# Four fused cross-attention layers on one core: row projection, weights cast in parts, masks moved between engines, three steps on GpSimd, new orders

## The reference

```
# layer 0: 16 heads of 8, causal (k < q, query 0 attends nothing)
x = layer_norm(x + softmax(mask(q k^T / sqrt(8))) v @ Wo + bo) * g1 + b1
x = layer_norm(x + relu(x @ W1 + b1) @ W2 + b2) * g2 + b2
# layer 1: 16 heads of 8, no mask, no norm
x = x + attention(x, ctx) @ Wo + bo
x = x + gelu_tanh(x @ W1 + b1) @ W2 + b2
# layer 2: gate; pooled = mean over tokens of ctx
vis = pooled @ Wv.T + bv;  text = x @ Wt.T + bt
route = softmax over tokens of 2 * sum(text * vis)
gate = sigmoid(text @ Wg_t.T + (route * vis) @ Wg_v.T + bg)
x = layer_norm(x + gate * route * vis) * gamma + beta
# layer 3: 16 heads of 64, on an rms-normed query
x = x + attention(rms_norm(x) * norm_w @ wq, ctx @ wk, ctx @ wv) @ wo
```

## Time and profile before

| | before |
|---|---|
| median of 3 runs | 1521.21 us |
| profiled execution: its span | 1521.7 us |
| PE busy | 1418.5 us (93%) |
| DVE busy | 1080.6 us (71%) |
| ACT busy | 977.0 us (64%) |
| POOL busy | 488.1 us (32%) |
| chain that ended last | PE 76%, DVE 10%, POOL 5%, ACT 4%, issue 4% |

### The profile page before, as it was taken

One profiled execution on the slowest core, in us unless ns is written; L12 is line 12 of the kernel. 1 busy time (PEld: TensorE's weight loads), 2 busy tenths in 40 slices (PEclk: granted clock), 3 DMA queues, 4 the chain that ended last, 5 costly groups with the idle time before them and its releaser, 6 DMA issues.

```text
span 1521.7 us, 48865 instructions
## 1 busy us (share of the span) xinstructions
PE 1418.5 (93%) x20325; PEld 1030.3 (68%) x20325; DVE 1080.6 (71%) x2644; ACT 977.0 (64%) x1877; POOL 488.1 (32%) x522
## 2 busy tenths in 40 slices
PE   4779999999999999999999999999999999999987
PEld 3455766767676676767667676776767667676756
DVE  4558778677786867778676777867687785776743
ACT  2355767667676766767576676767667676665654
POOL 2132523315242341524224252332424233152402
PEclk9999999999999999999999999999999999999998
DMA  4000000000000000000000000000000000000000
GB/s 141 15 2 15 3 8 16 9 16 2 22 3 9 16 9 16 3 22 3 9 16 9 16 3 22 3 9 16 9 16 3 9 16 9 2 3 8 3 8 9
DMA packets 27798, 20.02 MB, mean 13 GB/s; under 512 B 1088, under 2 KB 27200, under 8 KB 27328
## 3 DMA queue, kind: packets, MB, share of 16 engines
q1 hardware_dynamic: 27584, 16.90, 3.8%
HBM read 12.70 MB, written 4.19 MB: 11 GB/s over the span
## 4 chain that ended last, share of the span: by engine, by line
PE 76%; DVE 10%; POOL 5%; ACT 4%; issue 4%; DMA 0%; SPq 0%; ACTq 0%; DVEq 0%
PE bank L731 63%; PE bank L740 13%; DVE negmax L1261 2%; POOL prob L1157 2%; DVE sums L1408 2%; ACT prob L1096 1%; POOL rstd L1144 1%; DVE z L1319 1%; ACT probT L1031 1%; DVE negmax L1402 1%; DVE stats L1305 1%; POOL prob L1137 1%; POOL var_eps L1141 1%; POOL w_low L1128 0%; DVE mv L1310 0%
## 5 line engine op out<-in xcount | busy, mean ns | idle before, releaser
L1137 POOL TENSOR_TENSOR prob<-prob,rinv 128x512 f32<-128x512 f32 x256 | 262.4, 1044 | 369.1 <-DVE rinv L1268 368.7
L740 PE MATMUL bank<-cst,prob 128*128 128x128 f32 x1536 | 221.5, 277 | 14.5 <-POOL prob L1157 9.6
L740 PEld LDWEIGHTS bank<-cst,prob 128*128 128x128 f32 x1536 | 173.9, 141 | 62.5 <-issue 32.7
L1031 ACT ACTIVATE probT<-bank 128x512 f32<-128x512 f32 x256 | 143.8, 598 | 110.3 <-PE bank L740 109.4
L1261 DVE TENSOR_REDUCE negmax<-bank 128x8 bf16<-128x512 f32 x256 | 159.0, 680 | 70.7 <-PE bank L731 70.6
L1157 POOL TENSOR_TENSOR prob<-prob,rinv 128x512 f32<-128x512 f32 x128 | 132.5, 1042 | 230.0 <-DVE rinv L1412 229.7
L1024 ACT ACTIVATE prob<-bank 128x512 f32<-128x512 f32 x256 | 142.0, 608 | 80.3 <-PE bank L731 80.0
L1266 DVE TENSOR_REDUCE sums<-prob 128x8 f32<-128x512 f32 x256 | 169.2, 661 | 12.9 <-ACT prob L1024 11.0
L731 PE MATMUL bank<-negmax,ident_b 128*128 128x512 bf16 x384 | 129.6, 389 | 14.1 <-DVE negmax L1261 8.3
L731 PE MATMUL bank<-wt,Q 128*128 128x128 f32 x1024 | 126.1, 277 | 0.0
L1096 ACT ACTIVATE prob<-bank,rms_rows 128x256 f32<-128x256 f32 x256 | 104.5, 483 | 30.8 <-PE bank L731 30.7
(11 more groups left out here) (155 smaller groups left out, 2968.7 us busy)
## 6 DMA issues: line engine op xcount, KB each, us to landing
x_in<-in_x SPq DMA_DIRECT2D x16, 256.0 KB, 3.0
c_in<-in_ctx SPq DMA_DIRECT2D x16, 256.0 KB, 3.3
out<-y SPq DMA_DIRECT2D x16, 256.0 KB, 2.3
Q<-in_split_weights SPq DMA_DIRECT2D x1, 1536.0 KB, 9.1
wt<-in_weights SPq DMA_DIRECT2D x1, 1024.0 KB, 10.8
wt<-in_weights SPq DMA_DIRECT2D x1, 640.0 KB, 5.9
wt<-in_weights SPq DMA_DIRECT2D x4, 128.0 KB, 10.4
cst<-in_constants SPq DMA_DIRECT2D x1, 229.0 KB, 2.7
```

Source lines behind the costliest of these rows:

```text
L740: last = nc.tensor.transpose(o[:, k * P:(k + 1) * P], src(k), ident)
L1031: nc.scalar.activation(probT[:, t].rearrange("p s q -> p (s q)"), bank(g, "PT", l, u, t)[:, :], ACT.Identity).then_inc(probT_ready.sem, 1)
L1137: nc.gpsimd.tensor_tensor(pr, pr, ri, ALU.mult).then_inc(norm_ready.sem, 1)
```

## The change

- **Row projection.** `o.0` computes rows (tokens on partitions): four matmuls with 128 columns of `aT` as the stationary operand and `Wo0` as the moving one. A new POOL step `xb` adds the bias, spread over all rows, to the loaded rows `x_in`; `attout.0` adds that to the bank into `z[0]`, in rows. `lnT.0` is gone; `stats.0` and `z.0` read `z[0]` in SBUF. `ffn.0` writes `x1T[0]`. SP's load of group g + 1 also waits for `xb(g)`, and `xb(g)` for `attout.0` of the group before.
- **Weights in parts.** ACT casts `wk3` in step `c_high` and `wv3`, `wq3` one after the other in `qm.0`; DVE subtracts for `wk3` in `c_low`, POOL for the other two. `k3`, `v3`, `q3` wait each for its own part.
- **Masked keys by ACT.** Step `km` goes to ACT: two activations with scale and bias, the form of `qm`.
- **Masked values by copies.** `Vm` is zeroed once, and `vm` copies only the heads that the half keeps: two copies of 256 elements per partition.
- **Three steps on GpSimd**: `vis_route`, `y_gamma`, `y_beta`.
- **New orders**: all five lists, and a bank table for each of the 16 groups.

```diff
-TURN = 89.7521
+TURN = 88.5425
...
             def load(g):
...
                     sp.wait_ge(*cT_filled(g))
+                    sp.wait_ge(*xb_ready(g))
                     load(g + 1)
...
@@ PE, step "o" and text_weights
-                    mm(bank(g, "o", l)[:, :], w(f"Wo{l}"), aT[l][:, :, :].rearrange("p b q -> p (b q)"))\
-                        .then_inc(attout_filled.sem, 1)
+                    if l == 0:
+                        for k in range(CH):
+                            last = mm(bank(g, "o", 0)[:, k * P:(k + 1) * P],
+                                      aT[0][:, 2 * k:2 * k + 2, :].rearrange("p b q -> p (b q)"), w("Wo0"), start=(k == 0))
+                        last.then_inc(attout_filled.sem, 1)
...
+                mm(text_bank[:, 3 * P:4 * P], bo_columns, ident, start=False).then_inc(text_filled, 1)
...
@@ ACT
                 if kind == "c_high":
...
+                    if g == 0:
+                        act.wait_ge(split_rest_loaded, 16)
+                        cols = slice(SPLIT["wk3"], SPLIT["wk3"] + 2 * TOK)
+                        nc.scalar.activation(w_high[:, cols], staged(cols), ACT.Identity).then_inc(high_k3, 1)
...
                     if g == 0 and l == 0:
-                        act.wait_ge(split_rest_loaded, 16)
-                        rest = slice(FIRST_SPLIT, SPLIT_COLS)
-                        nc.scalar.activation(w_high[:, rest], w_stage[:, rest], ACT.Identity).then_inc(high_rest, 1)
+                        for name, high in (("wv3", high_v3), ("wq3", high_q3)):
+                            cols = slice(SPLIT[name], SPLIT[name] + 2 * TOK)
+                            nc.scalar.activation(w_high[:, cols], staged(cols), ACT.Identity).then_inc(high, 1)
+                elif kind == "km":
+                    l, = index
+                    act.wait_ge(*k_filled(g, l))
+                    if g and l == 0:
+                        act.wait_ge(*ffn_step(g - 1, 0, FT - 1))
+                    if g and l == 1:
+                        act.wait_ge(*fused_ready(g - 1))
+                    for k in range(2):
+                        last = nc.scalar.activation(Km[l][:, :, k, :], bank(g, "k", l)[:, :].rearrange("p (b k) -> p b k", b=GB),
+                                                    ACT.Identity, bias=bkm[:, l, k:k + 1], scale=m_c2[:, k:k + 1])
+                    last.then_inc(km_ready.sem, 1)
...
@@ POOL
+            pool.memset(Vm[:, :, :, :, :], 0.0).then_inc(vm_cleared, 1)
...
-            pool.wait_ge(high_rest, 1)
-            rest = slice(FIRST_SPLIT, SPLIT_COLS)
-            nc.gpsimd.tensor_tensor(w_low[:, rest], w_stage[:, rest], w_high[:, rest], ALU.subtract)\
-                .then_inc(low_rest, 1)
+            for name, high, low in (("wv3", high_v3, low_v3), ("wq3", high_q3, low_q3)):
+                cols = slice(SPLIT[name], SPLIT[name] + 2 * TOK)
+                pool.wait_ge(high, 1)
+                nc.gpsimd.tensor_tensor(w_low[:, cols], staged(cols), w_high[:, cols], ALU.subtract).then_inc(low, 1)
...
+                if kind == "xb":
+                    pool.wait_ge(x_loaded, 16 * (g + 1))
+                    if g == 0:
+                        pool.wait_ge(text_ready, 2)
+                    if g:
+                        pool.wait_ge(*attout_ready(g - 1, 0))
+                    nc.gpsimd.tensor_tensor(xb[:, :, :], x_in[:, :, :], bo_rows[:, :].unsqueeze(1).broadcast_to([P, CH, P]),
+                                            ALU.add).then_inc(xb_ready.sem, 1)
...
+                elif kind == "vis_route":
+                    pool.wait_ge(*vis_route_ready(g))
+                    pool.wait_ge(*gate_a(g))
+                    nc.gpsimd.tensor_tensor(seqs(route), seqs(route), over_tokens(vis_route[:, :]), ALU.mult)\
+                        .then_inc(route_ready.sem, 1)
+                elif kind == "y_gamma":
...
+                elif kind == "y_beta":
...
@@ DVE
-            for r in range(2):
-                rows = slice(64 * r, 64 * r + 64)
-                own = cst[rows, CCOL["m_v"]:CCOL["m_v"] + P]
-                dve.tensor_copy(m_vc[rows, r, :], own)
-                dve.tensor_scalar(m_vc[rows, 1 - r, :], own, -1.0, 1.0, ALU.mult, ALU.add)
...
+            for l in range(2):
+                dve.tensor_scalar(bkm[:, l, :], m_c2[:, :], v(f"bk{l}"), None, ALU.mult)
...
@@ step "c_low", group 0
+                        dve.tensor_copy(bo_columns, v("bo0").broadcast_to([P, P]))
...
+                        dve.tensor_copy(bo_rows[:, :], text_bank[:, 3 * P:4 * P])
...
+                        dve.wait_ge(high_k3, 1)
+                        cols = slice(SPLIT["wk3"], SPLIT["wk3"] + 2 * TOK)
+                        nc.vector.tensor_tensor(w_low[:, cols], staged(cols), w_high[:, cols], ALU.subtract).then_inc(low_k3, 1)
...
@@ step "vm"
                     for k in range(2):
-                        last = nc.vector.tensor_tensor(Vm[:, :, 2 * u:2 * u + 2, k, :], both,
-                                                       m_vc[:, k, :].unsqueeze(1).unsqueeze(1).broadcast_to([P, 2, 2, P]),
-                                                       ALU.mult)
+                        own = Vm[:, :, k, 2 * u:2 * u + 2, :].rearrange("p l j (n c d) -> p l (j n) c d", c=2, d=8)
+                        last = nc.vector.tensor_copy(own[:, :, :, k, :], both[:, :, :, k, :])
...
@@ step "attout", l = 0
-                    nc.vector.scalar_tensor_tensor(fT[l][:, :], bank(g, "o", l)[:, :], v(f"bo{l}"), (xT, x2T)[l][:, :],
-                                                   ALU.add, ALU.add).then_inc(attout_ready.sem, 1)
+                        dve.wait_ge(*xb_ready(g))
+                        nc.vector.tensor_tensor(z[0][:, :, :], bank(g, "o", 0)[:, :].rearrange("p (c f) -> p c f", c=CH),
+                                                xb[:, :, :], ALU.add).then_inc(attout_ready.sem, 1)
...
@@ steps "stats" and "z"
-                    dve.wait_ge(*lnT_filled(g, n))
+                    dve.wait_ge(*(lnT_filled(g, n) if n else attout_ready(g, 0)))
+                    rows = bank(g, "lnT", n)[:, :].rearrange("p (c f) -> p c f", c=CH) if n else z[0]
...
```

More of the change, by code:

```diff
@@ new lines @@
+TURN = 88.5425
+TILES = """
+    xT cT vis gv q.0 k.0 v.0 S.0.0.0 S.0.0.1 S.0.0.2 S.0.0.3 PT.0.0.0 PT.0.0.1 PT.0.0.2 PT.0.0.3 O.0.0.0 O.0.0.1 v.1
+    S.0.1.0 S.0.1.1 S.0.1.2 S.0.1.3 PT.0.1.0 PT.0.1.1 PT.0.1.2 PT.0.1.3 O.0.1.0 O.0.1.1 o.0 h.0.0 f.0 h.0.1 h.0.2
+    h.0.3 q.1 k.1 S.1.0.0 S.1.0.1 S.1.0.2 S.1.0.3 PT.1.0.0 PT.1.0.1 PT.1.0.2 PT.1.0.3 O.1.0.0 O.1.0.1 S.1.1.0 S.1.1.1
+    S.1.1.2 S.1.1.3 PT.1.1.0 PT.1.1.1 PT.1.1.2 PT.1.1.3 O.1.1.0 O.1.1.1 o.1 h.1.0 f.1 h.1.1 h.1.2 h.1.3 lnF.0 lnT.1
+    lnF.1 lnT.2 lnF.2 gp ag k3.0 v3.0 q3.0 k3.1 v3.1 q3.1 k3.2 v3.2 q3.2 k3.3 v3.3 q3.3 k3.4 v3.4 q3.4 k3.5 v3.5 q3.5
+    k3.6 v3.6 q3.6 k3.7 v3.7 q3.7 rows S3.0.0 S3.0.1 PT3.0.0 PT3.0.1 O3.0.0 O3.0.1 out3 S3.1.0 S3.1.1 PT3.1.0 PT3.1.1
+    O3.1.0 O3.1.1 S3.2.0 S3.2.1 PT3.2.0 PT3.2.1 O3.2.0 O3.2.1 S3.3.0 S3.3.1 PT3.3.0 PT3.3.1 O3.3.0 O3.3.1"""
@@ L374, in plan_of @@
+BANK = {g: dict(zip(TILES.split(), map(int, BANKS[g]))) for g in BANKS}
 def plan_of(group):
@@ L389, in program @@
     return [step[1:] for step in sorted(placed, key=lambda step: step[0])]
-PROGRAM = {engine: program(engine) for engine in PLAN}
+PROGRAM = {engine: program(engine) for engine in ("PE", "ACT", "DVE", "POOL")}
 class Signal:
@@ L554, in bank @@
         def bank(group, kind, *tile):
-            return psum[BANK[plan_of(group)][".".join([kind, *map(str, tile)])]]
+            return psum[BANK[group][".".join([kind, *map(str, tile)])]]
         xT_filled = Signal(sem("xT_filled"), "PE", "xT")
@@ L608, in xattn_sequence_kernel @@
         gv_ready = Signal(sem("gv_ready"), "DVE", "gv")
-        km_ready = Signal(sem("km_ready"), "DVE", "km")
+        km_ready = Signal(sem("km_ready"), "ACT", "km")
         vm_ready = Signal(sem("vm_ready"), "DVE", "vm")
@@ L629, in xattn_sequence_kernel @@
         gate_b = Signal(sem("gate_b"), "DVE", "gate_pre")
-        route_ready = Signal(sem("route_ready"), "DVE", "vis_route")
+        route_ready = Signal(sem("route_ready"), "POOL", "vis_route")
         gate_c = Signal(sem("gate_c"), "DVE", "fuse")
         fused_ready = Signal(sem("fused_ready"), "DVE", "fuse")
-        y_gamma_ready = Signal(sem("y_gamma_ready"), "DVE", "y_gamma")
-        y_ready = Signal(sem("y_ready"), "DVE", "y_beta")
+        y_gamma_ready = Signal(sem("y_gamma_ready"), "POOL", "y_gamma")
+        y_ready = Signal(sem("y_ready"), "POOL", "y_beta")
         yn_ready = Signal(sem("yn_ready"), "DVE", "yn")
@@ L1084, in step @@
                     if g == 0:
-                        act.wait_ge(low_rest, 1)
+                        for low in (low_k3, low_v3, low_q3):
+                            act.wait_ge(low, 1)
                     if g:
@@ L1238, in step @@
                         .then_inc(gv_ready.sem, 1)
-                elif kind == "km":
-                    l, = index
```

(5 more changed lines are left out.)

743 lines of the change are left out of this document (383 added, 360 removed).

## The result

Four runs of the changed kernel gave a median of 1500.33 us (1496.36 to 1501.57), against 1521.9 us for four of the kernel before: a ratio of 0.986, 95% interval 0.9841 to 0.9878, or 21.6 us. Measured again on another chip the ratio was 0.9851 (0.983 to 0.9873). The forecast was 1499.

The account below looks back on a forecast made before the run. The prediction took PE, busy 93% of the span, as the bound: its work plus its idle time. From 1521.7 us it took 6.0 (work), 3.8 (start), 3 (26 to 100 us) and 9.5 (middle), forecasting 1499 us, range 1479 to 1515.

Parts of the forecast that it names:

- PE work, −6.0: PE's matmul work: −6.0 us, from `lnT.0` gone (−6.9), `o.0`'s new form (+0.6) and bias rows (+0.3).
- The start, −3.8: Before 26 us: first scores at 23.9 instead of 27.99, PE's idle time down by 3.8 us; bounds 0 and 8.
- 26 to 100 us, −3: Group 0 nearly alone, its chain exposed: −3 us of PE's 19.3 us idle, between +3 and −10.
- The middle, −9.5: PE's waits in the long middle: 12.5 us saved at three places, 3 given back for new steps; bounds −25, +33.
- (a) `z`: `lnF.0`'s wait for `z.0`, covered by steps standing between `o.0` and `lnF.0`: 6 of 8.9 us gone.
- (b) `probT`: `O.1.0`'s wait for `probT`, with 16 records of `out3.1` now ahead of it: −3.5 of 4.9 us.
- (c): PE's wait for POOL's layer 3 probabilities, with two shifts instead of one between `PT3.0.0` and `PT3.0.1`: −3 of 9.6 us.
- The end, 0: Last group, without filler: its gate chain loses nothing, `vis_route` running beside the last add and tanh; 0 within ±2 us.
- The rule on SBUF: DVE instructions with two SBUF inputs and GpSimd reading SBUF exclude each other: 38 us of DVE, sum unchanged.
- The first (only removed work counts, 1512): Gains at PE's waits and up to 100 us come back elsewhere; removed work and start remain: 1512 us, chance 0.17.
- The second, GpSimd as the gate: Two of four new POOL steps per group exposed ahead of `norm`, `rstd` and `rms`: 1542 us, chance 0.08.
- The other two, 1477 us and 1517 to 1526: Idle time halved in the middle and up to 100 us: 1477 us, chance 0.13; both sides cancel: 1517 to 1526, 0.07.

Follow-up runs that it names:

- row projection alone: The kernel before with only `o.0` computed into rows, the residual added from GpSimd's `xb`, and no `lnT.0`: 1515.66 us, ratio 0.9955.
- second profile of the changed kernel: The changed kernel measured once more, unaltered, on one chip beside later runs: 1500.47 us, ratio 0.9851 to the kernel before.
- The splitting alone: The kernel before with only the second-stage weights in parts (`wk3` first, then `wv3` and `wq3`): 1510.67 us, ratio 0.9918.
- All parts in the old orders: The changed code with the step orders and group period of the kernel before, moved steps placed: 1536.77 us, ratio 1.0101.
- 48 twins more: The changed kernel with an idle copy ahead of each of GpSimd's three new 128x512 steps, 48 more instructions: 1526.86 us, ratio 1.0045.
- 48 steps taken back: The changed kernel with `vis_route`, `y_gamma` and `y_beta` back on VectorE, `xb` staying on GpSimd: 1515.83 us, ratio 0.9956.

## Why the prediction came out, step by step

**PE work, −6.0: the right sign, too small.** `o.0` came out as priced: 0.89 us from its start to the next in the row projection alone, 0.81 in the changed kernel, against 0.90. But PE is busy 0.68 us less in each full-clock turn of the row projection alone, and 0.65 less in the changed kernel, where my −6.9 and +0.6 make 0.39 a turn. That is 10 to 11 us in 16 groups instead of 6.3, within the 5 us that the split into busy and idle is good for. What the difference consists of, no row tells. In the whole profile PE is busy 14.5 us less, outside the 5 to 10 that I gave as a sign (8.7 in the second profile of the changed kernel).

**The start, −3.8: right,** 3.4 us measured, and the scores at 24.17 against 23.9. What I gave as its cause holds only in part. The splitting alone is worth 13 us in before's order and 1 to 3 us in the new one; the new order had queued `c_low` ahead of `xT` and two casts ahead of `km.0`, and so spent most of it.

**26 to 100 us, −3: 2.4 measured,** at a mean granted clock of 0.89 of full speed instead of 0.93. The agreement says little. In the second profile of the changed kernel, at 0.77, PE idled 16.7 us there, as little as in the first, and yet its first `out` came 6.5 us later: it was busy for 57.3 us with 520 records, where the first had 57.1 us with 606.

**The middle, −9.5: the turn right, its composition wrong.** With the removed work I had 15.5 us for 16 groups, 0.97 a turn; measured 1.05. The two terms are off in opposite directions: by the busy times 0.65 a turn is work (forecast 0.38) and 0.40 is idle time (forecast 0.59), so that part of the agreement is luck. (a) `z` and (b) `probT` went wholly, 6.0 and 3.8 us in eleven turns, and (c) fell by 2.8, as forecast. I gave back 3 us; what came up in their place was 13 (issue 7.3, negmax 5.7). The net 4.4 us came out of gaps too short for a row of their own: all rows together, some small ones with them, make 26.9 us of 32.5 before and 27.6 of 28.1 after. So the waits that I had picked out did go, and it was not their going that shortened the idle time.

**The end, 0: 4.3 us lost.** The last turn takes 63.32 us instead of 59.07, although it was granted a clock of 0.92 and before's 0.88. All parts in the old orders have 58.99, so that it is the new lists for the last groups that cost this, not the steps moved: every kernel here with the new orders takes 62.5 to 65.0 us for this turn, every one with the old 56.9 to 59.1. In the sum it is hidden by the turn of group 13, 4.0 us shorter.

**Not forecast:** the second turn, 6.2 us shorter where I had 1, by the work that the new orders pull ahead. Up to the first `out` the gain was 2 us more than my terms, and behind the twelfth group 0.8 were lost where they had some 3 of gain. In sum that is the 4.6 us by which the two profiles lie further apart than my sum had them; the changed kernel's profile is its shortest run. That the medians, 21.6 us apart, come so near to the forecast's 22.3 is in good part luck: errors of 3 to 5 us in single terms cancel.

**The other engines.** DVE is busy 991 us and POOL 557, near the forecast's 982 and 555; for POOL two errors cancel, 1273 ns a step for three of the four instead of 1042, and one of three subtractions now on DVE. ACT is busy 1002 us, not 1023.

**The rule on SBUF: borne out in this step, and harmless.** `agree`, that had 1236 ns in the median, has 1419 now:

```profile
L1407 DVE TENSOR_TENSOR room<-x1T,gv x16: 691/1419/1478, 113.0 to 1437.6; 128x512 f32<-128x512 f32 x16
```

The 64 new GpSimd steps are not the reason. With all of them in the old orders the median is 1236 ns, and in the new orders it is 1420 with 48 twins more as with 48 steps taken back. What counts is the normalisation that GpSimd has under way when `agree` starts. In the middle of the changed kernel four of them run up to 819.17 + 4.05 = 823.22, and `agree` ends 0.55 us behind that, at 823.77; in the middle of before the two ends are 839.27 and 839.81. Only the last group's `agree` has no GpSimd instruction beside it:

```profile
819.17 4.05 POOL L1202 TENSOR_TENSOR prob<-prob,rinv 128x512 f32<-128x512 f32 x4 [16.48 <-DVE rinv L1341]
...
822.35 1.42 DVE L1407 TENSOR_TENSOR room<-x1T,gv 128x512 f32<-128x512 f32 x1
...
1437.56 0.69 DVE L1407 TENSOR_TENSOR room<-x1T,gv 128x512 f32<-128x512 f32 x1
```

And where `agree` came first, at 1290.15 in before, it took 0.65 us, and the product that GpSimd had started 0.16 us behind it took 1.39 instead of 1.04. By the rule (the Trainium skill, "SBUF — State Buffer", "Who interferes with whom") the one of the two that comes later waits; these rows agree. The new orders make `agree` start earlier in the last of these products, 0.17 us behind its start instead of 0.34, and that costs 3 us of VectorE in all, off the bound.

**The rivals.** The first (only removed work counts, 1512) was far too kind to the old orders: with them, and the moved steps placed by hand, the parts cost 15 us. The second, GpSimd as the gate, did not come true, but a cost of that kind is near: the next 50.8 us of GpSimd cost 28, though by way of ScalarE's squares and not of the norms that the rival had. The first 57, in the orders of before, cost next to nothing, and the same steps taken back cost 15. My argument against this rival, that GpSimd is idle for 63%, was no reason; that its steps stood in gaps was. The other two, 1477 us and 1517 to 1526, lie outside the measured interval.

What the forecast rested on without saying so is that someone had written orders fit for the parts. Parts and orders can't be priced apart: the orders are worth some 36 us with these parts, against the one placing by hand that was measured, and the four parts that were measured alone −13 to +24 us each without them. Which of the changes of order brings how much was not taken apart.
